# A new merge table for two interleaved groups of boards, and a new lag between them

## The chip, the core and the metric

The kernel runs on one NeuronCore of a Trainium2 chip. The time is that of the device for one launch, in microseconds (us), and lower is better. The engines are named as in the profile: PE is TensorE's matrix multiply, PEld its weight loads, DVE is VectorE, ACT is ScalarE, POOL is GpSimd, SP is the queue that issues DMAs.

## What is computed

128 boards of 64 squares with 256 features pass through four residual layers. Each begins with a layer norm and a ReLU. Layers 0, 1 and 3 are masked attention, layer 2 is a gated graph layer with a tanh.

```python
h = jnp.maximum(_layernorm(x, axis=-1), 0.0)
x = x + _L0_gnn_ref(h, adj, adj, ...)   # 8 heads, six static masks, two from adj
h = jnp.maximum(_layernorm(x, axis=-1), 0.0)
x = x + _L1_gnn_ref(h, adj, ...)        # 4 heads, mask adj
h = jnp.maximum(_layernorm(x, axis=-1), 0.0)
x = x + _L2_gnn_ref(h, adj, ...)        # below
h = jnp.maximum(_layernorm(x, axis=-1), 0.0)
x = x + _L3_gnn_ref(h, adj, ...)        # as layer 1
...
# attention: softmax(where(mask, q k^T * scale, -big)) v, then Wo and bias
# layer 2:
Wh = jnp.einsum('bni,hoi->bhno', h, W) + bW[None, :, None, :]
e = jnp.einsum('bhno,hop->bhnp', Wh, attn)
A_mat = jnp.tanh(jnp.where(adj[:, None], jnp.einsum('bhnp,bhmp->bhnm', e, Wh), 0.0))
hp = jax.nn.relu(jnp.einsum('bhnm,bhmo->bhno', A_mat, Wh))
ha = cat(hp) @ A_w.T ; hf = h @ fc_w.T
coeff = jax.nn.sigmoid(hf @ g1_w.T + ha @ g2_w.T + gbias)
return hf * coeff + ha * (1.0 - coeff)
```

## The kernel before

A group is four boards, 256 rows. Two groups are in flight, in two sets of buffers called slot 0 and slot 1; in tile names the last digit is the slot (`xn1` is slot 1's). There are 32 groups, so 16 turns of both slots: the first turn is written out, the other 15 are one hardware loop (`passes`, line 321), and the rest of slot 1 follows it. Below, one trip of that loop is a pass.

A group's work is a list of 111 steps, `STEPS`: attention layer 0 (here A0), attention layer 1 (A1), the graph layer (L2), attention layer 3 (A3). Every engine walks the same list and does its share of each step. The steps that matter here:

- `bn`, `stats`, `norm`: the layer norm. DVE takes the statistics (line 928 reads x, then 935 and 938), POOL raises to the power -0.5 (line 405), DVE writes the normalised `xn` (line 946).
- `turn`: PE transposes `xn` (line 500); ACT writes the rounded half `hT` (line 760), DVE the rest (line 960). Each fp32 product is taken as three products of such halves, so a consumer waits for both.
- `q`, `k`, `v`, `scores`; then `mask` and `max` on DVE, the exponentials on ACT (line 785, named `max` there too), `soft` on DVE (lines 1014, 1016). A1 and A3 have two units of softmax each, A0 has four.
- `pt` transposes the probabilities on PE (line 577), ACT copies them (line 792). `pv` multiplies them with v on PE; ACT and DVE write the two halves of `oT` (lines 795, 867). `out` is the output projection; DVE adds x (line 1025).
- L2: `r` (four row terms of the scores; DVE line 1045, then POOL spreads them over a 128x1024 tile `row_terms`, line 410), `e` for four heads (ACT line 813, DVE line 1050), `s2` scores and tanh, `a` (halves of the masked tanh, and their row sums), `ah`, `hp` for four heads, `ha`, `hf`, `hat` (transposes, line 711), `g` and `sum` the gate. In `hat` POOL also adds 128x512 numbers to x (line 418).

The order of the two slots on one engine is written out by hand as a table, `ORDER`. It has a number for every step: after step k of slot 0, so many steps of slot 1 are done. The lag says how many of these, at the start of a turn, still belong to slot 1's previous group. There is a table for PE, ACT, DVE and POOL each; SP has its own fixed order, in which the next `x` of a slot is loaded when `res` says that A3's `out` has been added (line 1025). Waits are on semaphores, so any order that doesn't deadlock gives the same numbers, and PE executes its list strictly as it stands. No planner decides anything when the kernel runs.

Within a pass, slot 0's L2 runs beside slot 1's A0, and slot 1's L2 beside slot 0's A0; the A1 of one slot runs beside the A3 of the other. "First half" is from slot 0's A0 `turn` to slot 1's A0 `turn` (slot 1 finishes its L2 and A3 in it), "second half" the rest of the pass.

Of the kernel before, what the change touches and what calls it, by code (L numbers as in the profile page):

```python
# [58 lines left out]
def constants():  # L59
# [22 lines left out]
    for part in (0, LO):  # L82
# [11 lines left out]


ORDER = {
# [5 lines left out]
    "act": (44, (  # L102
# [4 lines left out]
    "dve": (49, (  # L107
# [4 lines left out]
    "pool": (41, (  # L112
# [4 lines left out]
}  # L117


# [1017 lines left out]
```

## Time and profile before

| | |
|---|---|
| median of three runs | 2304.79 us (2302.14 to 2306.58) |
| the profiled execution, as timed | 2314.06 us |
| its span in the trace | 2311.9 us |
| PE busy in the span | 2106.4 us, 91% |
| PEld, DVE, ACT, POOL busy | 81%, 63%, 50%, 8% |
| mean granted TensorE clock | 0.979 of full speed |

The profiled execution is 9.3 us longer than the median of the runs, of which 2.2 us lie outside its span. The table of the span by slices shows PE at nine tenths or more nearly throughout; only the first slices (weights and their products are set up, about 100 us) and the last (one slot alone) have less. A busy PE is an upper figure: the matmuls overlap and their ends are modelled. Idle time before a group is put down to whatever ended it, and "issue" means that the profile shows nothing that was waited for.

### The profile page before, as it was taken

How to read it: one execution, taken by the hardware profiler on the slowest of the kernel's cores; microseconds unless marked ns; L12 is line 12 of the kernel's file. 1: busy time of each engine (PE TensorE's matmuls, PEld its weight loads, DVE VectorE, ACT ScalarE, POOL GpSimd, SP SyncE). 2: the span in 40 equal slices, each digit the busy share in tenths (PEclk: the TensorE clock that was granted, in tenths of full speed). 3: DMA queues.
4: the chain of work that ended last, by engine and by line, in shares of the span. 5: the costliest groups of instructions: out<-in, count | busy, mean ns of one | idle time of the engine just before them, and what ended most of it. 6: DMA issues, size and time to landing. Idle time of an engine off the chain costs nothing.

```text
span 2311.9 us, 53587 instructions
## 1 busy us (share of the span) xinstructions
PE 2106.4 (91%) x21228; PEld 1875.6 (81%) x21228; DVE 1466.1 (63%) x3769; ACT 1160.4 (50%) x3862; POOL 192.5 (8%) x203
## 2 busy tenths in 40 slices
PE   6799999999999999999999999999999999999997
PEld 5688888888887888888888887888888888888886
DVE  4466666666666666667666666666667666666663
ACT  3355454455454555455455455455455455455452
POOL 0000101100101100101100100110100100100100
PEclk8799999999999999999999999999999999999998
DMA  5000000000000000000000000000000000000000
GB/s 169 1 9 5 11 12 11 12 11 2 12 11 12 10 11 3 11 12 11 12 11 2 12 11 12 11 11 3 11 12 11 12 11 2 12 11 12 10 6 5
DMA packets 40644, 30.89 MB, mean 13 GB/s; under 512 B 15664, under 2 KB 40240, under 8 KB 40432
## 3 DMA queue, kind: packets, MB, share of 16 engines
q1 hardware_dynamic: 40432, 27.48, 4.1%
q8 instruction: 204, 3.34, 0.6%
q14 instruction: 8, 0.07, 0.0%
HBM read 19.08 MB, written 8.39 MB: 12 GB/s over the span
## 4 chain that ended last, share of the span: by engine, by line
PE 71%; DVE 11%; ACT 11%; issue 4%; DMA 3%; POOL 1%; SPq 0%; DVEq 0%; POOLq 0%; ACTq 0%
PE ps L432 66%; ACT probs L785 5%; PE ps L577 3%; DVE xn L946 2%; PE ps L500 2%; DMA x<-x 2%; DVE wide L1050 2%; ACT oT L795 1%; DVE small L928 1%; DVE probs L1016 1%; ACT probsT L792 1%; DVE aT L867 1%; ACT hT L760 1%; POOL small L405 1%; DMA raw_mats<-mats 1%
## 5 line engine op out<-in xcount | busy, mean ns | idle before, releaser
L432 PE MATMUL ps<-hT,w_hi 128*128 128x256 f32 x2560 | 499.0, 288 | 9.8 <-ACT hT L760 9.6
L432 PEld LDWEIGHTS ps<-hT,w_hi 128*128 128x128 f32 x2560 | 409.5, 190 | 24.8 <-ACT hT L760 18.4
L785 ACT ACTIVATE probs<-probs,small 128x64 f32<-128x64 f32 x1024 | 341.4, 338 | 77.6 <-DVE small L1006 76.2
L432 PE MATMUL ps<-hT,w_lo 128*128 128x256 f32 x1280 | 336.6, 283 | 0.0
L432 PE MATMUL ps<-w_hi,hT 128*128 128x256 f32 (+1 forms) x1024 | 249.0, 312 | 0.0
L432 PEld LDWEIGHTS ps<-hT,w_lo 128*128 128x128 f32 x1280 | 243.6, 190 | 2.0
L432 PE MATMUL ps<-wide,w_hi 128*128 128x256 f32 x1024 | 218.3, 287 | 3.1
L432 PE MATMUL ps<-w_hi,oT 128*128 128x256 f32 x768 | 187.5, 309 | 31.3 <-DVE oT L867 17.0
L405 POOL TENSOR_TENSOR small<-small,consts 128x2 f32<-128x2 f32 x128 | 88.8, 694 | 1420.7 <-DVE small L938 1420.7
L785 ACT ACTIVATION_READ_ACCUMULATOR probs<-probs,small 128x1 f32 x1024 | 195.2, 191 | 0.0
L432 PEld LDWEIGHTS ps<-w_hi,hT 128*128 128x128 f32 x1024 | 174.9, 188 | 8.4
L432 PE MATMUL ps<-w_hi,cT 128*128 128x256 f32 x768 | 169.3, 298 | 10.9 <-ACT cT L845 8.2
L432 PEld LDWEIGHTS ps<-wide,w_hi 128*128 128x128 f32 x1024 | 164.3, 188 | 17.1 <-ACT wide L830 12.5
L432 PEld LDWEIGHTS ps<-w_hi,oT 128*128 128x128 f32 x768 | 143.8, 203 | 41.2 <-DVE oT L867 40.4
L867 DVE TENSOR_TENSOR oT<-ps,oT 128x256 fp32r<-128x256 f32 x192 | 80.9, 424 | 151.5 <-ACT oT L795 149.4
L760 ACT ACTIVATE hT<-ps 128x256 fp32r<-128x256 f32 x256 | 85.4, 382 | 135.1 <-PE ps L500 134.4
L813 ACT ACTIVATE wide<-ps,c_vec 128x256 fp32r<-128x256 f32 x256 | 107.5, 471 | 88.5 <-PE ps L432 88.5
L432 PEld LDWEIGHTS ps<-w_hi,cT 128*128 128x128 f32 x768 | 126.6, 188 | 28.5 <-ACT cT L845 15.8
L432 PE MATMUL ps<-w_lo,hT 128*128 128x256 f32 (+1 forms) x512 | 149.6, 309 | 0.0
L432 PEld LDWEIGHTS ps<-kT,qT 64*64 64x64 f32 (+1 forms) x4096 | 125.3, 133 | 24.2 <-issue 15.4
L432 PE MATMUL ps<-kT,qT 64*64 64x64 f32 (+1 forms) x4096 | 142.8, 222 | 0.0
L946 DVE TENSOR_SCALAR xn<-x,small 128x256 f32<-128x256 f32 x256 | 120.8, 513 | 23.7 <-POOL small L405 22.5
(123 smaller groups left out, 4454.7 us busy)
## 6 DMA issues: line engine op xcount, KB each, us to landing
raw_mats<-mats SPq DMA_DIRECT2D x8, 1024.0 KB, 11.9
x<-x SPq DMA_DIRECT2D x32, 256.0 KB, 2.9
out<-xn SPq DMA_DIRECT2D x32, 256.0 KB, 3.1
adj<-adjq SPq DMA_DIRECT2D x64, 16.0 KB, 2.0
adjT<-adjt SPq DMA_DIRECT2D x64, 8.0 KB, 2.1
raw_consts<-board_consts SPq DMA_DIRECT2D x1, 451.5 KB, 3.2
raw_rows<-rows SPq DMA_DIRECT2D x1, 256.0 KB, 4.5
bias_cols<-cols SPq DMA_DIRECT2D x1, 6.0 KB, 3.9
```

The costliest lines, as they stand in the source:

```text
L405: nc.gpsimd.tensor_tensor(RSTD[s], VE[s], HALF.broadcast_to([P, TT]), ALU.pow).then_inc(sm["rstd"], 1)
L432: return nc.tensor.matmul(o, lhsT, rhs, start=start, stop=stop, skip_group_check=True)
L500: last = nc.tensor.transpose(bank(s, H_BANKS[c])[:, t * P:t * P + P], XN[s][:, t * D + c * P:t * D + c * P + P], IDENT)
L577: last = nc.tensor.transpose(bank(s, 1 - i)[:, at:at + P], PR[s][:, j, at:at + P], IDENT)
L760: fn(HT[s][:, 0, c, :], bank(s, H_BANKS[c])[:, 0:TOK], ACT.Relu).then_inc(S[s]["hT_hi"], 1)
L785: last = fn(p, p, ACT.Exp, bias=ROWMAX[s][:, row:row + 1], accum_out=ROWSUM[s][:, row:row + 1])
L792: fn(PTS[s][:, j, at], bank(s, 1 - i)[:, at], ACT.Copy).then_inc(sm["pt_sb"], 1)
L795: fn(OT[s][:, 0, i, :].rearrange("p (t e q) -> p t e q", t=TT, e=2), o_view(s, i), ACT.Copy).then_inc(sm["oT_hi"], 1)
L813: last = fn(e_view(s, 0, oc, i), e_bank(s, E_BANKS[i], oc), ACT.Identity, bias=CVEC[:, oc, i:i + 1])
L867: return tt(o, full, hi.bitcast(F32), ALU.subtract)
L946: ts(XN[s][:, t * D:t * D + D], X[s][:, t * D:t * D + D], MV[s][:, t, 0:1], RSTD[s][:, t:t + 1], ALU.subtract, ALU.mult).then_inc(S[s]["xn ...
L1050: stt(e_view(s, 1, oc, i), e_bank(s, E_BANKS[i], oc), CVEC[:, oc, i:i + 1], e_view(s, 0, oc, i).bitcast(F32), ALU.add, ALU.subtract).then_ ...
```

## The change

The four tables of `ORDER` and their lags are replaced; nothing else is touched. Lags go from 44, 44, 49, 41 (PE, ACT, DVE, POOL) to 50, 48, 48, 51. A row of the table as an example; the other rows change in the same manner.

```diff
 ORDER = {
-    "pe": (44, (
-        0, 0, 0, 0, 0, 0, 2, 0, 0, 1, 0, 0, 0, 3, 0, 0, 0, 0, 2, 1, 0, 0, 0, 0, 1, 2, 0, 1, 0, 2, 0, 0, 1,
...
+    "pe": (50, (
+        1, 2, 0, 0, 2, 1, 2, 0, 1, 3, 0, 0, 0, 5, 1, 0, 0, 0, 0, 0, 0, 0, 0, 0, 0, 0, 0, 1, 0, 1, 0, 0, 3,
...
```

What it does in a pass, by the steps of each engine's list:

- PE, both halves: L2's `a` for the first tile comes after the other slot's A0 `k` (it was after `v` in the first half and before `k` in the second). In the first half the four A0 `scores` move behind `ah`; in the second they stood there already.
- PE, both halves: A1's `turn` comes before the other slot's `g`, not behind it. In the first half A0's `out` moves ahead of the last `ha`.
- PE, both halves: A3's first `pt` comes before A1's `out` of the other slot. ACT does the first A3 unit of exponentials before A1's `pv`, and DVE does A3's masks, maxima and first `soft` before A1's `pv`.
- The jump of the loop moves in every list. On PE it stood between slot 1's last `e` and slot 0's A0 `turn`; now it stands behind slot 0's last A3 `out`, ahead of slot 1's `r` and `e`. Slot 1's L2 `turn` comes before that last `out`.
- POOL, slot 1: `row_terms` comes behind slot 0's A0 power. In both halves DVE does `r` and the first head of `e` before A0's `bn` of the other slot, and A3's `out` of one slot behind L2's `turn` of the other, not before it.

POOL's list, from the last rows ahead of the loop (0 and 1 are the slots; `small` holds the norm's statistics). Before:

```order
L410 TENSOR_TENSOR row_terms1<-rs1,consts 128x1024
L321 UNCONDITIONAL_BRANCH
L321 ISA
L405 TENSOR_TENSOR small0<-small0,consts 128x2
L418 TENSOR_TENSOR x1<-x1,f1 128x512
```

And now, from the same place:

```order
L321 UNCONDITIONAL_BRANCH
L321 ISA
L405 TENSOR_TENSOR small0<-small0,consts 128x2
L410 TENSOR_TENSOR row_terms1<-rs1,consts 128x1024
L404 REGISTER_ALU
```

Slot 1's `row_terms` has moved across the jump and stands right behind the power of slot 0's norm, as slot 0's stands behind slot 1's in the middle of the pass (unchanged).

DVE's list in the middle of a pass, from slot 0's L2 `norm`. Before:

```order
L946 TENSOR_SCALAR xn0<-x0,small0 128x256 x2
L1025 TENSOR_TENSOR xn1<-ps,x1 128x256 x2
L960 SCALAR_TENSOR_TENSOR hT0<-ps,hT0 128x256 x2
L928 BN_STATS small1<-x1 128x6
L1044 REGISTER_ALU
L1045 SCALAR_TENSOR_TENSOR rs0<-ps,s0,rs0 4x256
L928 BN_STATS small1<-x1 128x6
L935 BN_AGGR small1<-small1 128x2 x2
L938 TENSOR_SCALAR small1<-small1 128x2
L1050 SCALAR_TENSOR_TENSOR wide0<-ps,c_vec,wide0 128x4x64 x4
L946 TENSOR_SCALAR xn1<-x1,small1 128x256 x2
```

Now:

```order
L946 TENSOR_SCALAR xn0<-x0,small0 128x256 x2
L960 SCALAR_TENSOR_TENSOR hT0<-ps,hT0 128x256 x2
L1025 TENSOR_TENSOR xn1<-ps,x1 128x256 x2
L1044 REGISTER_ALU
L1045 SCALAR_TENSOR_TENSOR rs0<-ps,s0,rs0 4x256
L1050 SCALAR_TENSOR_TENSOR wide0<-ps,c_vec,wide0 128x4x64 x2
L928 BN_STATS small1<-x1 128x6 x2
L935 BN_AGGR small1<-small1 128x2 x2
L938 TENSOR_SCALAR small1<-small1 128x2
L1050 SCALAR_TENSOR_TENSOR wide0<-ps,c_vec,wide0 128x4x64 x2
L946 TENSOR_SCALAR xn1<-x1,small1 128x256 x2
```

A3's `out` of slot 1 and with it the next load of `x1` move behind two `hT0`, and the statistics of `x1` move behind `rs0` and two of the four `wide0`.

PE's list at the end of a pass, from slot 0's second A3 `pt`, as it now is:

```order
L577 MATMUL ps<-consts,probs0 128x128 x2
L585 REGISTER_ALU
L432 MATMUL ps<-probsT0,v0 64x64 x8
...
L432 MATMUL ps<-bias_rows,sel_rows 128x256
L500 MATMUL ps<-consts,xn1 128x128 x4
L432 MATMUL ps<-w_hi,oT0 128x256
...
L321 COMPARE_AND_BRANCH
```

Before, the four transposes of `xn1` stood behind both halves of `out`, `r` and `e` followed them, and the jump came only behind `e`:

```order
L500 MATMUL ps<-consts,xn1 128x128 x4
L432 MATMUL ps<-hT1,u_vec 36x256 x6
...
L432 MATMUL ps<-hT1,w_hi 128x256 x2
L321 REGISTER_ALU
L321 COMPARE_AND_BRANCH
```

## Rows read from the trace of the kernel before

**Rows 1.** The page: engine, busy us, share, instructions; clock by slices.

```profile
PE 2106.4 (91%) x21228; PEld 1875.6 (81%) x21228; DVE 1466.1 (63%) x3769; ACT 1160.4 (50%) x3862; POOL 192.5 (8%) x203
...
PEclk8799999999999999999999999999999999999998
```

**Rows 2.** Stretches: busy us of each engine, granted clock, DMA share, GB/s.

```profile
core 0: us, PE busy (x) PEld busy (x) DVE busy (x) ACT busy (x) POOL busy (x), PEclk, DMA share, GB/s
870.55:1008.31 137.76, 127.42 (x1317) 113.63 (x1317) 90.13 (x235) 71.25 (x240) 11.87 (x12) 1.00 0.04 10
591.99:731.85 139.86, 130.19 (x1317) 116.23 (x1317) 90.54 (x236) 71.24 (x240) 11.89 (x12) 0.98 0.04 10
...
718.87:722.28 3.41, 2.94 (x14) 2.94 (x14) 1.95 (x6) 0.38 (x1) 0.69 (x1) 0.50 0.00 0
715.46:718.87 3.41, 2.18 (x40) 1.33 (x38) 2.80 (x12) 2.23 (x11) 0.00 (x0) 1.00 0.00 0
```

**Rows 3.** PE's waits, pass 870.55 to 1008.31: waiter, releaser, us, times, longest.

```profile
PE ps L500 <- issue: 3.2, 2, 1.7
PE ps L577 <- DVE probs L1016: 2.5, 5, 0.9
PE ps L500 <- DVE xn L946: 1.2, 1, 1.2
```

**Rows 4.** The loop's line: duration ns min/median/max, first and last start.

```profile
L321 PEldq COMPARE_BRANCH  x15: 83/3498/3848, 311.8 to 2250.0; - x15
...
L321 PEldq COMPARE_BRANCH  x1: 3498/3498/3498, 1004.6 to 1004.6; - x1
```

**Rows 5.** PE in order of time (start, us, what, idle before), around the jump.

```profile
999.93 1.10 PE L432 MATMUL ps<-hT,u_vec 128*36 128x256 f32 x6 [0.26 <-ACT hT L760]
...
1006.39 0.40 PE L432 MATMUL ps<-hT,w_hi 128*128 128x256 f32 x2
1008.31 0.56 PE L500 MATMUL ps<-consts,xn 128*128 128x128 f32 x3 [1.52 <-issue]
```

**Rows 6.** POOL and DVE in order of time, in the middle of the pass.

```profile
936.60 0.69 POOL L405 TENSOR_TENSOR small<-small,consts 128x2 f32<-128x2 f32 x1 [7.54 <-DVE small L938]
937.26 1.91 POOL L410 TENSOR_TENSOR row_terms<-rs,consts 128x1024 fp32r<-128x1024 f32 x1
...
972.99 1.28 POOL L418 TENSOR_TENSOR x<-x,f 128x512 f32<-128x512 f32 x1
...
934.53 0.43 DVE L928 BATCH_NORM_STATS2 small<-x 128x6 f32<-128x256 f32 x1 [2.46 <-DMA x<-x]
...
936.56 1.66 DVE L1050 SCALAR_TENSOR_TENSOR wide<-ps,c_vec,wide 128x256 fp32r<-128x256 f32 x4
938.13 1.51 DVE L946 TENSOR_SCALAR xn<-x,small 128x256 f32<-128x256 f32 x2
```

**Rows 7.** ACT and PE, A1 and A3 late in the pass; a group of the page.

```profile
989.82 0.66 ACT L792 ACTIVATE probsT<-ps 128x256 f32<-128x256 f32 x2 [1.05 <-PE ps L577]
...
L785 ACT ACTIVATE probs<-probs,small 128x64 f32<-128x64 f32 x1024 | 341.4, 338 | 77.6 <-DVE small L1006 76.2
...
991.75 0.39 PE L432 MATMUL ps<-w_hi,oT 128*128 128x256 f32 x1 [0.65 <-DVE oT L867]
...
995.36 0.44 PE L577 MATMUL ps<-consts,probs 128*128 128x128 f32 x2 [0.89 <-DVE probs L1016]
...
997.31 0.39 PE L432 MATMUL ps<-w_hi,oT 128*128 128x256 f32 x1 [0.47 <-ACT oT L795]
```

**Rows 8.** PE in order of time: `hat`, `g`, and behind them A1's `q`.

```profile
973.34 0.60 PE L711 MATMUL ps<-consts,f 128*128 128x128 f32 x4
974.19 0.39 PE L432 MATMUL ps<-w_hi,cT 128*128 128x256 f32 x1 [0.26 <-ACT cT L845]
...
977.31 0.39 PE L432 MATMUL ps<-hT,w_hi 128*128 128x256 f32 x1 [0.31 <-ACT hT L760]
```

**Rows 9.** PE in order of time: `a` of the second tile, first half.

```profile
881.36 1.05 PE L432 MATMUL ps<-aT,sel_rows 128*128 128x512 f32 x2
```

More of the change, by code:

```diff
@@ L96 @@
 ORDER = {
[5 rows of a table removed]
-    "act": (44, (
[4 rows of a table removed]
-    "dve": (49, (
[4 rows of a table removed]
-    "pool": (41, (
[4 rows of a table removed]
[5 rows of a table added]
+    "act": (48, (
[4 rows of a table added]
+    "dve": (48, (
[4 rows of a table added]
+    "pool": (51, (
[4 rows of a table added]
 }
```

30 rows, old and new, of the table ORDER are left out of this document.

## The prediction

> **What bounds the kernel now.** Read the page first. PE is busy 91% of the span [rows 1], no other engine passes 81%, and PE's own work is the same before and after: the change only permutes it. So the question is how much of PE's idle time goes or comes. Next take one pass of the loop that ran at full clock, 870.55 to 1008.31: 137.76 us with PE busy for 127.42 [rows 2]. About 10.3 us of idle time per pass, times 15 passes, is all that an order can win: 155 us at the very most. The waits of that pass [rows 3] say where it lies: ahead of transposes of `xn` (3.2 and 1.2 us), ahead of transposes of probabilities (2.5 us), and in a dozen waits of 0.2 to 0.7 us for halves of `hT`, `oT` and `cT`. Then I read these places in order of time, with ACT, DVE and POOL beside PE. Of each place I ask how long the chain that ends the wait is, and how much PE work the new order puts over it. Three facts of the trace carry what follows.
>
> First, the jump of the loop is dear on PE alone. It took 3.5 us in the median (15 times, the 83 ns is the last, which is not taken) [rows 4]. In this pass it began at 1004.6, while the last matmul before it began at about 1006.5, and PE went on at 1008.31 after 1.52 us idle [rows 5]. So the sequencer was some 2.2 us ahead of its engine and hid that much of the jump. The matmuls in that stretch follow each other every 0.12 us, so it was ahead by about 18 of them, or 36 instructions with their weight loads.
>
> Second, `norm` on DVE is held up by POOL. `row_terms` ran from 937.26 to 939.17; the two `norm` issued at 938.13 took 1.51 us together where 0.74 is the rule, and the first ended only when POOL had ended [rows 6]. By itself one takes 0.41.
>
> Third, the clock. In the pass 591.99 to 731.85 it fell twice, and the pass took 139.86 instead of 137.76 us [rows 2]: 1.05 us for each fall. Before the fall at 718.87 PE had done 40 short matmuls with gaps, 2.18 us busy of 3.41; then the clock was 0.50, that is 1.2 instead of 2.4 GHz. I count 11 such falls in the 15 passes.
>
> **The change part by part**, per pass, minus is a gain.
>
> (a) `a`, `ah`, `scores`, `hp`. In the first half the second `a` took 1.05 us [rows 9] where 0.63 would do, and `hp` waited some 0.65 us behind `ah` for the halves of `ah`'s result. The new order puts 64 small matmuls (1.9 us) over the second wait. It shortens the cover of the second `a` from the scores (1.9 us) to `v` (14 matmuls of 0.12, 1.7 us); against it stand a copy of the row sums, one of `aT` (0.6 each) and DVE's half (0.7), so about 0.3 us stay open. In the first half the exponentials of A0 now stand before `hp`'s first ReLU on ACT (4 x 0.338 = 1.35 us [rows 7]), and `ha` pays 0.35 of it. First half -0.5. In the second half the first `a` loses a wait of 0.5 us and gets the 0.3 of the second: -0.3. Sum **-0.8** (bounds -1.4 and 0).
>
> (b) `turn` before `g`. Now PE waits 0.26 behind `hat`, then runs `g`, `turn`, waits 0.31, and reaches `q` 3.97 us after `hat` (973.34 to 977.31) [rows 8]. After: `norm` in this place is itself held by POOL's addition (972.99 to 974.27 [rows 6]), so `turn` starts about 1.1 us after `hat`; its four transposes and `g` (1.6 us) then cover every copy, and `q` starts after 3.4. Second half -0.55. In the first half `norm` came after the addition and `q` after 3.49 us; it now takes the second half's form: -0.1. Sum **-0.65** (-1.0 to -0.2).
>
> (c) A3's first `pt` between A1's `pv` and `out`, first half. ACT starts A3's exponentials right behind the two copies of rows 7 (989.82 + 0.66) instead of behind A1's `pv`, 1.4 us earlier, but A1's `pv` copies now wait 1.35 us for them, so PE idles 1.45 us ahead of A3's `pt` instead of 0.65 ahead of A1's `out` (991.75). In exchange the second `pt` loses its 0.89 (995.36) and the whole chain to L2's `r` ends 0.7 us sooner: **-0.7** (-1.2 to 0).
>
> (d) The middle of the pass. DVE now adds A3's `out` of slot 1 after two `hT`, which sends the load of `x1` 1.0 to 1.9 us later, and does `rs` and two `wide` before `bn`. `bn` starts 1.45 us later than the 934.53 of rows 6, with 0.5 less between it and the power. The power ends 0.95 us later, `row_terms` follows it at once as now, and `norm`, with only two `wide` between, meets it whole: its first half ends with `row_terms`, near 940.3 on that pass's clock, not 939.5. PE waited 1.2 us here [rows 3] and will wait about 2.1: **+0.9** (0 to +1.5).
>
> (e) The end of the pass. Slot 0's A3 has the pattern of (c), but DVE has `bn` and `stats` of L2 before A3's `pv`; I find A3's first `out` starting 7.6 us after A1's `pt` (989.34), where it is 7.97 (997.31 [rows 7]). Then PE waits 0.4 us for `xn1`, does `turn` and the second `out` (1.2 us). The sequencer has 36 instructions from that first `out` to the jump, so it reaches the jump as `out` begins, and `r` can start 3.5 + 0.2 us later: 11.4 us after `pt`, where `r` at 999.93 came after 10.59 [rows 5]. That is +0.8 up to here. Behind `e` the jump's 1.52 us are gone, but POOL now does slot 1's `row_terms` (1.92 us) between the power and `norm`. The power ends 6.4 us after `r`, `row_terms` 8.3, and PE's A0 `turn` starts 8.45 after `r`; it was 1008.31 - 999.93 = 8.38. What the jump gave back the hold takes. Sum **+0.85** (-0.6 to +2.1).
>
> The sum is -0.8 - 0.65 - 0.7 + 0.9 + 0.85 = -0.4 us per pass, 15 passes: -6 us. The clock: sparse stretches on PE around A1 and A3 get longer but fewer. I take as many falls as now, but they come to lie over `out`'s dense matmuls at 14 x 0.12 more, 0.3 us dearer: +3 us (0 to +12). The first turn and the tail have one slot alone on PE and keep their order: 0. So the profiled 2311.9 would be 2309, and the median of 2304.8 becomes **2302 us**. A measurement of this kernel tells about 0.2% (4.6 us) from no change.
>
> On (d) and (e) the Trainium skill bears, page SBUF — State Buffer, section "SBUF: two separate sides": the port pair that VectorE and GpSimd share is an exclusive lock, and whichever starts first holds it for its whole instruction. By this rule the 1.92 us are lost whole. The trace agrees, with 15 of 15 `norm` under `row_terms` lengthened from 0.41 to 1.19. On the jump in (e), the Trainium skill's page TensorE: Matmul & The Clock Gate, "Architectural detail: the array is 16× 32×32, not 1× 128×128", gives TensorE's queue a depth of 64. By that, the sequencer would be 32 matmuls or 3.8 us ahead and today's jump would be hidden whole; the trace shows 2.2 us ahead and 1.52 open, so the measurement decides.
>
> **The rivals.** *The hold does not come about (faster).* If DVE's `norm` gets in before `row_terms`, (d) turns from +0.9 to about -0.6 and (e) from +0.85 to about -0.5: with the rest -3.2 per pass, 2260 us. For it: POOL's start and DVE's lie only 0.1 us apart. Against it: the same pair with the addition of line 418 in place of `row_terms` starts 0.08 us apart, and there POOL was first in 16 of 16. *The fills count in full (faster).* (a) to (c) reach 0.3 us more each, or (e) comes out even: -1.3 per pass, 2286 us. For it: DVE and ACT are idle 37% and 50%. *The jump lies bare (slower).* If the sequencer does not run past the wait for `xn1`, it reaches the jump only 8.9 us after `pt`, and `r` starts after 12.6 instead of 11.4: +1.2 per pass, and with the longer gap a fall of the clock in every second pass. That gives +0.8 per pass plus 4 to 6 us: 2321 us. It decides from the point where less than 3.5 us of PE work stands between the sequencer's arrival at the jump and the last matmul ahead of it; now there are 2.2, then 2.4 with a wait inside. *The order doesn't reach the end at all:* each gain is eaten by the next wait of the same pass, 2305.
>
> **How the numbers follow.** The sum as worked, 2302 with its own range of 2292 to 2312: 0.45, of which 0.18 faster by over 0.2%, 0.22 within, 0.05 slower. The jump bare: 0.22. Fills in full: 0.15. No hold: 0.10. Nothing: 0.08. Faster 0.43, same 0.30, slower 0.27. The range 2280 to 2325 leaves out the no-hold case and the far end of the bare jump.
>
> **What would show it.** PE's idle ahead of line 500 in the middle of a pass at 2 us (d), and again at 1.3 to 1.6 before slot 0's, put down to `xn` and no longer to "issue". DVE's `norm` at 2.0 us under `row_terms` 30 times instead of 1.19 15 times. The jump still 3.5 us, with some 1.2 us open ahead of `r`. No wait of `q` for `hT` behind `g`, no 0.89 ahead of the second A3 `pt`, one of 1.4 ahead of the first. The prediction is wrong if POOL's `row_terms` doesn't meet `norm`, or if PE's idle ahead of `r` is over 2.5 us.

## The result, and the profile after

| | before | after |
|---|---|---|
| median | 2303.47 us (2301.18 to 2306.58, 4 runs) | 2340.77 us (2337.04 to 2342.48, 4 runs) |
| the profiled execution, as timed | 2314.06 us | 2341.77 us |
| its span | 2311.9 us | 2339.6 us |
| mean granted TensorE clock | 0.979 | 0.964 |

The changed kernel takes 1.0159 times as long as the kernel before, with a 95% interval of 1.0140 to 1.0177: **slower by 1.6%**, and outside the predicted range of 2280 to 2325.

First the page of the kernel after, its lines of busy times and of the chain, and two groups (line, engine, shape, count, busy us, mean ns, idle before it). They answer to [rows 1].

```profile
PE 2096.4 (90%) x21228; PEld 1890.3 (81%) x21228; DVE 1502.8 (64%) x3769; ACT 1145.4 (49%) x3862; POOL 190.7 (8%) x203
...
PE 71%; DVE 14%; issue 8%; ACT 4%; POOL 2%; DMA 1%; DVEq 0%; SPq 0%; ACTq 0%; POOLq 0%
...
L946 DVE TENSOR_SCALAR xn<-x,small 128x256 f32<-128x256 f32 x256 | 169.8, 704 | 45.6 <-POOL small L405 41.4
L500 PE MATMUL ps<-consts,xn 128*128 128x128 f32 x512 | 108.9, 306 | 84.0 <-DVE xn L946 84.0
```

PE has the same 21228 matmuls as before. DVE is busy 37 us longer: line 946, the `norm` that POOL holds up, grew by 49 us (from 120.8 to 169.8), and the rest of DVE's work is 12 us shorter. The span grew by 27.7 us; the medians lie 37.3 apart. The profiled execution of before was 9.3 us above the median known then, so the traces explain 27 of the 37 us; for the other 10 there is no trace of a typical execution of the kernel before.

PE's waits inside the loop (180 to 2230 us; waiter, releaser, us in total, times, longest), first the kernel before:

```profile
PE ps L577 <- DVE probs L1016: 37.0, 73, 0.9
PE ps L500 <- issue: 21.9, 14, 1.8
PE ps L432 <- ACT hT L760: 15.2, 53, 0.3
```

and after:

```profile
PE ps L500 <- DVE xn L946: 64.7, 58, 2.0
PE ps L577 <- DVE probs L1016: 40.8, 29, 1.4
PE ps L432 <- issue: 37.1, 28, 2.6
```

This is the heart of the case. Before, idle time is spread over many waits of at most 1.2 us, but for the 14 of 1.3 to 1.8 us that the jump leaves ahead of slot 0's A0 `turn`. Now the 29 waits for probabilities are 1.4 us each, those for `xn` ahead of A0's `turn` reach 2.0 us, and the bare jump of 2.2 to 2.6 us stands in every pass (14 of the 28 put down to "issue"; the others are of 0.3 us).

Next the places of the prediction. The middle of a pass, POOL, DVE and PE in order of time, answering to [rows 6]:

```profile
947.82 0.69 POOL L405 TENSOR_TENSOR small<-small,consts 128x2 f32<-128x2 f32 x1 [7.74 <-DVE small L938]
948.47 1.91 POOL L410 TENSOR_TENSOR row_terms<-rs,consts 128x1024 fp32r<-128x1024 f32 x1
...
948.62 2.23 DVE L946 TENSOR_SCALAR xn<-x,small 128x256 f32<-128x256 f32 x2
...
950.59 1.22 PE L500 MATMUL ps<-consts,xn 128*128 128x128 f32 x4 [1.98 <-DVE xn L946]
```

`row_terms` starts right behind the power, and the pair of `norm` takes 2.23 us instead of 0.74. The end of the pass (PE, and the loop's line), answering to [rows 4, 5, 7]:

```profile
1001.21 0.66 PE L577 MATMUL ps<-consts,probs 128*128 128x128 f32 x4
...
1008.76 0.38 PE L432 MATMUL ps<-w_hi,oT 128*128 128x256 f32 x1 [0.87 <-DVE oT L867]
...
1009.70 0.79 PE L500 MATMUL ps<-consts,xn 128*128 128x128 f32 x4
...
1013.61 0.90 PE L432 MATMUL ps<-hT,u_vec 128*36 128x256 f32 x6 [2.28 <-issue]
...
1021.83 0.87 PE L500 MATMUL ps<-consts,xn 128*128 128x128 f32 x4 [1.63 <-DVE xn L946]
...
L321 PEldq COMPARE_BRANCH  x1: 3354/3354/3354, 1010.1 to 1010.1; - x1
```

The sequencer reached the jump at 1010.1, 8.9 us behind A1's `pt`, 1.34 us behind the first matmul of A3's `out` (1008.76, which had waited for `oT`) and 0.4 us behind the start of `turn`, and PE stood idle for 2.28 us. Last, stretches of PE with the granted clock as seventh figure (us, busy of each engine, clock, DMA share, GB/s), behind the waits for `xn` of three halves, and one just behind the first of them, answering to [rows 2]:

```profile
882.70:886.10 3.40, 3.40 (x9) 2.58 (x8) 2.79 (x8) 0.60 (x1) 0.00 (x0) 0.50 0.02 5
886.10:889.50 3.40, 3.40 (x27) 3.22 (x26) 1.56 (x3) 1.12 (x2) 0.00 (x0) 1.00 0.00 0
950.90:954.30 3.40, 3.40 (x11) 2.81 (x11) 3.09 (x8) 0.38 (x1) 0.00 (x0) 0.51 0.00 0
1022.60:1026.00 3.40, 3.40 (x10) 2.65 (x10) 2.63 (x7) 0.89 (x3) 0.00 (x0) 0.50 0.02 5
```

PE was never idle in the first, third and fourth, but ran `s2` at 1.2 GHz: 9 to 11 matmuls, where an experiment below has 14 of them in such a stretch with 0.35 us to spare. The clock record of the trace has **31 such falls between the first and the last A0 `turn` of the loop, where the kernel before has 11**. Of the 31, 18 begin within 1.4 us of A0's `turn`, 6 around A3's first `pt` and 7 around the bare `r`. Of the 11 before, ten begin 1.5 to 2.7 us behind the second A3 `pt`, which waits 0.89 us among other short waits, and only one behind the 14 waits of 1.3 to 1.8 us at the jump. So the length of a wait does not decide by itself.

### Where the time went

I cut each half of a pass at five marks on PE: A0's `turn`, `hat`, A1's `pt`, `r` and the next A0's `turn`. Of each piece I took the median over those of the loop's 15 or 14 halves in which the clock did not fall, in us:

| piece | before, first half | after | before, second half | after | term |
|---|---|---|---|---|---|
| A0's `turn` to `hat` | 34.48 | 33.92 | 33.96 | 33.86 | (a) |
| `hat` to A1's `pt` | 15.52 | 15.30 | 16.01 | 15.32 | (b) |
| A1's `pt` to `r` | 10.71 | 9.78 | 10.58 | 12.40 | (c), (e) |
| `r` to A0's `turn` | 7.88 | 8.70 | 8.42 | 8.20 | (d), (e) |
| sum | 68.59 | 67.70 | 68.97 | 69.78 | |

At full clock a pass takes 137.56 before and 137.48 us after: the new order by itself changes nothing. The 14.5 passes between the marks would take 1994.4 and 1992.4 us; they took 2007.4 and 2034.4. What is left over is 13.0 us for 11 falls and 42.0 us for 31 falls, 1.2 and 1.35 us each. So -2 us are the order and +29 us the clock, together the 27 us by which the two traces differ.

### The profile page after: what moved, and what is told of

Read it like the earlier page. It is cut to its first block, busy times and chain, and to the rows that moved or that the text cites. A ratio compares the mean times of both kernels' runs of the same rounds, so it can differ in the third digit from the quotient of the medians.

```text
span 2339.6 us, 53632 instructions
## 1 busy us (share of the span) xinstructions
PE 2096.4 (90%) x21228; PEld 1890.3 (81%) x21228; DVE 1502.8 (64%) x3769; ACT 1145.4 (49%) x3862; POOL 190.7 (8%) x203
## 4 chain that ended last, share of the span: by engine, by line
PE 71%; DVE 14%; issue 8%; ACT 4%; POOL 2%; DMA 1%; DVEq 0%; SPq 0%; ACTq 0%; POOLq 0%
PE ps L432 65%; DVE xn L946 4%; PE ps L500 4%; PE ps L577 2%; DVE small L928 2%; ACT probs L785 2%; POOL small L405 2%; DVE x L1025 1%; DVE aT L867 1%; DVE rs L867 1%; DVE small L935 1%; DVE wide L1050 1%; ACT rs L826 1%; ACT probsT L792 1%; DVE probs L1016 1%
## 5 line engine op out<-in xcount | busy, mean ns | idle before, releaser
L432 PE MATMUL ps<-hT,w_hi 128*128 128x256 f32 x2560 | 493.5, 287 | 0.2
L432 PE MATMUL ps<-wide,w_hi 128*128 128x256 f32 x1024 | 212.3, 284 | 0.2
L946 DVE TENSOR_SCALAR xn<-x,small 128x256 f32<-128x256 f32 x256 | 169.8, 704 | 45.6 <-POOL small L405 41.4
L500 PE MATMUL ps<-consts,xn 128*128 128x128 f32 x512 | 108.9, 306 | 84.0 <-DVE xn L946 84.0
L432 PE MATMUL ps<-w_hi,cT 128*128 128x256 f32 x768 | 159.9, 290 | 0.3 <-ACT cT L845 0.3
L500 PEld LDWEIGHTS ps<-consts,xn 128*128 128x128 f32 x512 | 59.6, 144 | 120.0 <-DVE xn L946 111.3
```

Of the source, the lines that this page charges most:

```text
L432: return nc.tensor.matmul(o, lhsT, rhs, start=start, stop=stop, skip_group_check=True)
L500: last = nc.tensor.transpose(bank(s, H_BANKS[c])[:, t * P:t * P + P], XN[s][:, t * D + c * P:t * D + c * P + P], IDENT)
L946: ts(XN[s][:, t * D:t * D + D], X[s][:, t * D:t * D + D], MV[s][:, t, 0:1], RSTD[s][:, t:t + 1], ALU.subtract, ALU.mult).then_inc(S[s]["xn ...
```

## The experiments

The kernels ran in three groups, each on one chip and with the kernel before beside it, which took 2312.9 to 2315.5 us there; ratios are to that. The changed kernel itself ran only on the first chip, beside 2303.5 us, so between it and the others the traces are the safer comparison: they give somewhat less than the ratios (31 and not 39 us from the changed kernel to a_pejump). All kernels do the whole computation. "Full clock" is the sum of the table above made for that kernel, for 14.5 passes (before 1994.4, after 1992.4), "falls" are counted as above. The expectations count them over a slightly longer stretch: 32, 28 and 17 for the changed kernel, a_pejump and a_both. a_fill has no full-clock sum, because in every one of its second halves the clock falls around `r`.

| kernel | ratio (95% interval) | full clock | traced | falls |
|---|---|---|---|---|
| after | 1.0159 (1.0140 to 1.0177) | 1992.4 | 2034.4 | 31 |
| a_pejump | 0.9991 (0.9970 to 1.0013) | 1964.7 | 2003.2 | 27 |
| a_rtfirst | 0.9914 (0.9887 to 0.9941) | 1954.1 | 1990.0 | 25 |
| a_both | 0.9751 (0.9723 to 0.9778) | 1932.0 | 1952.0 | 14 |
| a_both_ptfill | 0.9673 (0.9657 to 0.9689) | 1934.7 | 1935.6 | 1 |
| b_rtlate | 1.0013 (0.9996 to 1.0030) | 1994.5 | 2008.1 | 10 |
| b_rtfirst | 0.9999 (0.9986 to 1.0012) | 1995.6 | 2007.5 | 8 |
| b_ab | 0.9918 (0.9901 to 0.9934) | 1968.0 | 1991.6 | 17 |
| b_c2 | 1.0011 (0.9992 to 1.0030) | 1992.6 | 2013.4 | 19 |
| b_c | 1.0079 (1.0051 to 1.0106) | 1997.3 | 2022.6 | 23 |
| b_pejump | 1.0088 (1.0056 to 1.0120) | 2011.6 | 2028.9 | 12 |
| a_fill | 1.0087 (1.0065 to 1.0108) | none | 2028.2 | 20 |
| a_pejump_fill | 1.0073 (1.0050 to 1.0096) | 2000.4 | 2027.9 | 15 |

### The jump: a_pejump and b_pejump

a_pejump is the changed kernel with five steps of PE moved back across the jump:

```diff
-    "pe": (50, (
-        1, 2, 0, 0, 2, 1, 2, 0, 1, 3, 0, 0, 0, 5, 1, 0, 0, 0, 0, 0, 0, 0, 0, 0, 0, 0, 0, 1, 0, 1, 0, 0, 3,
+    "pe": (45, (
+        0, 0, 0, 0, 0, 1, 2, 0, 1, 3, 0, 0, 0, 5, 1, 0, 0, 0, 0, 0, 0, 0, 0, 0, 0, 0, 0, 1, 0, 1, 0, 0, 3,
...
-        0, 0, 5, 0, 0, 0, 2, 4, 0, 0, 2, 0)),
+        0, 0, 5, 0, 0, 0, 2, 4, 0, 0, 2, 5)),
```

> The changed kernel with the loop's jump of PE alone put back behind slot 1's last e (lag 50 to 45, five steps L2 r and e0 to e3 moved back across the jump); ACT, DVE, POOL and the order of PE's steps stay as changed. Theory A (the clock): the extra 36 us of the changed kernel are mostly its 32 falls of the granted clock instead of 11, of which about 7 begin at r behind the bare jump. PE's idle ahead of r falls from 3.9 to under 1.5 us, the hold of xn by row_terms stays at both halves: 1.0 us per pass for the idle and 7 falls at 1.65 us, so 2341 - 15 - 12 = 2314 us with some 25 falls. Theory B (idle time alone; falls cost nothing since they lie beside waits): 2341 - 15 = 2326 us whatever the count of falls. Theory C (the order of A1 and A3, not the jump, costs the time): 2336 to 2341 us.

Measured 0.9991, 1.7% below the changed kernel by the ratios and 31 us by the traces; I had expected 27. The same place, and the loop's line:

```profile
985.44 0.66 PE L577 MATMUL ps<-consts,probs 128*128 128x128 f32 x4
...
995.42 0.86 PE L432 MATMUL ps<-hT,u_vec 128*36 128x256 f32 x6
...
1003.74 0.90 PE L500 MATMUL ps<-consts,xn 128*128 128x128 f32 x4 [1.76 <-DVE xn L946]
...
L321 PEldq COMPARE_BRANCH  x1: 3578/3578/3578, 999.8 to 999.8; - x1
```

`r` follows `pt` after 9.98 us instead of 12.40, and the jump ends at 1003.4, under the wait for `xn` that is there anyway. The full-clock sum is 27.7 us shorter, and four falls are gone.

b_pejump is the reverse: the kernel before, with only PE's jump moved ahead of `r`.

```diff
-    "pe": (44, (
-        0, 0, 0, 0, 0, 0, 2, 0, 0, 1, 0, 0, 0, 3, 0, 0, 0, 0, 2, 1, 0, 0, 0, 0, 1, 2, 0, 1, 0, 2, 0, 0, 1,
+    "pe": (50, (
+        6, 0, 0, 0, 0, 0, 2, 0, 0, 1, 0, 0, 0, 3, 0, 0, 0, 0, 2, 1, 0, 0, 0, 0, 1, 2, 0, 1, 0, 2, 0, 0, 1,
...
-        0, 0, 0, 0, 1, 12, 0, 0, 1, 0, 0, 8)),
+        0, 0, 0, 0, 1, 12, 0, 0, 1, 0, 0, 2)),
```

> The kernel before with the loop's jump of PE alone moved ahead of slot 1's r (lag 44 to 50, L2 r and e0 to e3 behind the jump); all else as before. The jump then lies behind the transposes of xn1 and is bare. Theory A: idle ahead of r grows by 1.5 us, the 1.52 us ahead of slot 0's A0 turn shrinks by 0.9, so +0.6 us per pass, +9 us, and the clock falls at r in every second pass, 7 x 1.05 = 7 us: 2305 + 16 = 2321 us with 16 to 20 falls. Theory B (idle time alone): 2314 us. Theory C (the place of the jump makes no difference, its 3.5 us only change places): within 3 us of 2305.

Measured 1.0088 (1.0056 to 1.0120), 20 us; theory A had 1.007, B 1.004 and C 1.000.

```profile
1008.16 0.39 PE L432 MATMUL ps<-w_hi,oT 128*128 128x256 f32 x1 [0.47 <-ACT oT L795]
...
1009.92 0.60 PE L500 MATMUL ps<-consts,xn 128*128 128x128 f32 x4
1013.06 1.49 PE L432 MATMUL ps<-hT,u_vec 128*36 128x256 f32 x6 [2.54 <-issue]
...
L321 PEldq COMPARE_BRANCH  x1: 3451/3451/3451, 1009.4 to 1009.4; - x1
```

`r` comes 12.86 us behind `pt` (at 1000.20), 2.3 us later than before. At full clock `r` to A0's `turn` is 2.0 us shorter in exchange (6.42 us, from the two passes without a fall there), but A0's `turn` to `hat` behind it is 0.7 us longer, which I can't explain. The full-clock sum is 17 us above the kernel before, of the 21.5 us between the two traces. The loop has 12 falls where the kernel before has 11, and they now begin around `r`. So most of what the jump costs here is idle time and not the clock.

### The hold: a_rtfirst, b_rtlate, b_rtfirst

a_rtfirst is the changed kernel with POOL's `row_terms` ahead of the other slot's A0 power, in both halves:

```diff
-        0, 0, 0, 0, 0, 0, 0, 1, 0, 2, 0, 0, 0, 0, 0, 1, 0, 4, 0, 3, 0, 0, 0, 1, 0, 0, 0, 0, 0, 0, 0, 0, 0,
-        0, 0, 0, 1, 0, 0, 5, 0, 3, 0, 0, 0, 0, 0, 0, 3, 0, 27, 0, 0, 0, 0, 0, 0, 2, 1, 2, 0, 29, 0, 0, 3, 0,
+        0, 2, 0, 0, 0, 0, 0, 0, 0, 1, 0, 0, 0, 0, 0, 1, 0, 4, 0, 3, 0, 0, 0, 1, 0, 0, 0, 0, 0, 0, 0, 0, 0,
+        0, 0, 0, 1, 0, 0, 5, 0, 3, 0, 0, 0, 0, 0, 0, 3, 0, 27, 0, 0, 0, 0, 0, 0, 2, 0, 0, 0, 32, 0, 0, 3, 0,
```

> The changed kernel with POOL's row_terms ahead of the power of the other slot's A0 norm, in both halves; nothing else. norm is then no longer held by row_terms. Theory A (the clock): xn comes about 0.85 us sooner, 30 times, 26 us, and the some 20 falls of the clock that begin right behind the wait ahead of A0's turn go with their idle time, 20 x 1.65 = 33 us: 2341 - 26 - 33 = 2282 us, with some 12 falls. Theory B (idle time alone): 2341 - 26 = 2315 us. Theory C (row_terms only changes places with the power, which then comes as much later): within 5 us of 2341, and PE's waits ahead of line 500 stay near 2 us.

Measured 0.9914, 44 us below the changed kernel by the traces and already faster than the kernel before.

```profile
923.22 1.92 POOL L410 TENSOR_TENSOR row_terms<-rs,consts 128x1024 fp32r<-128x1024 f32 x1 [3.86 <-DVE rs L1045]
927.02 0.69 POOL L405 TENSOR_TENSOR small<-small,consts 128x2 f32<-128x2 f32 x1 [1.88 <-DVE small L938]
...
928.29 0.87 PE L500 MATMUL ps<-consts,xn 128*128 128x128 f32 x4 [0.41 <-DVE xn L946]
```

Here nobody meets anybody: `row_terms` has ended 1.88 us before the power can begin, and `r` to A0's `turn` goes from 8.70 to 7.34 us in the first half and from 8.20 to 6.72 in the second. The 18 falls behind this wait are gone, all of them. But 31 became only 25, not the 12 I expected: 17 now begin around A3's first `pt` instead of 6, and 8 around the bare `r` instead of 7. The gain is idle time, 38 us at full clock, more than theory A's 26, and 6 us of clock.

b_rtlate puts only slot 1's `row_terms` across the jump in the kernel before (the first of POOL's rows; the last two change with it):

```diff
-    "pool": (41, (
-        0, 1, 0, 0, 0, 0, 1, 0, 2, 1, 0, 0, 0, 1, 0, 0, 1, 0, 0, 1, 0, 0, 0, 2, 0, 0, 0, 0, 0, 3, 0, 0, 6,
+    "pool": (50, (
+        0, 0, 10, 0, 0, 0, 1, 0, 2, 1, 0, 0, 0, 1, 0, 0, 1, 0, 0, 1, 0, 0, 0, 2, 0, 0, 0, 0, 0, 3, 0, 0, 6,
...
```

b_rtfirst moves only slot 0's ahead of the power:

```diff
-        0, 11, 0, 0, 0, 0, 0, 0, 4, 0, 0, 0, 0, 0, 0, 2, 0, 0, 0, 0, 2, 1, 0, 1, 0, 7, 0, 2, 2, 0, 2, 0, 0,
+        0, 11, 0, 0, 0, 0, 0, 0, 4, 0, 0, 0, 0, 0, 0, 2, 0, 0, 0, 0, 2, 1, 0, 1, 0, 3, 0, 0, 8, 0, 2, 0, 0,
```

> The kernel before with slot 1's row_terms on POOL moved across the jump, behind the power of slot 0's A0 norm (POOL's lag 41 to 50); all else as before. norm of slot 0 is then held by row_terms as slot 1's is in the middle. Theory A: PE's jump covers the hold, since power ends 6.4 us and row_terms 8.3 us after r, and A0's turn started 8.38 us after r anyway: +0.1 us per pass, 2306 us (2303 to 2310), falls 11 to 14. Rival: the hold adds to the jump, +1.0 us per pass and a fall in every second pass at A0's turn: 2305 + 15 + 8 = 2328 us.

> The kernel before with POOL's row_terms of slot 0 ahead of the power of slot 1's A0 norm in the middle of the pass; nothing else. norm in the middle is then held by nobody. Theory A: r to A0's turn 7.74 us in the middle becomes 7.1 to 7.3 (the changed kernel went from 8.70 to 7.34), 15 times 0.5 us and no more falls: 0.9965 of the kernel before. Theory B (the wait ahead of A0's turn is set by the load of x1 and bn, not by norm): 1.000.

Measured 1.0013 and 0.9999. The first is as theory A had it: behind `e` the jump of 3.5 us covers the hold. In the second theory A failed (it had 0.9965). In the kernel before, `row_terms` ahead of the power gains nothing:

```profile
933.60 1.91 POOL L410 TENSOR_TENSOR row_terms<-rs,consts 128x1024 fp32r<-128x1024 f32 x1 [6.14 <-DVE rs L1045]
935.62 0.69 POOL L405 TENSOR_TENSOR small<-small,consts 128x2 f32<-128x2 f32 x1
...
934.40 1.13 DVE L938 TENSOR_SCALAR small<-small 128x2 f32<-128x2 f32 x1
```

The hold has only changed its place: DVE's line 938, which writes what the power needs, starts at 934.4, beside `row_terms`, takes 1.13 us instead of 0.17 and ends with it, and the power follows then. The old order does the first `bn` before `r`, the new one `r` and the first `e` before `bn`. In a_rtfirst, with the new order on DVE, POOL is idle for 1.88 us between `row_terms` and the power. So it is the change's own part (d) that makes the room for `row_terms`; the change only left `row_terms` on the wrong side of the power.

### Both at once: a_both

Its edits are the two shown of a_pejump and a_rtfirst, on PE:

```diff
-    "pe": (50, (
+    "pe": (45, (
...
```

and the two rows of POOL's table.

> The changed kernel with both parts undone that were undone one by one so far: PE's jump back behind slot 1's last e, and POOL's row_terms ahead of the power in both halves. One by one they gave 0.9991 and 0.9914 of the kernel before, where the changed kernel had 1.0159. Theory A (they add up, since the jump lengthens the way to r and the hold the way to A0's turn): 1.0159 - 0.0168 - 0.0245 = 0.975, some 2256 us on a chip that gives 2313 for the kernel before. Theory B (behind e the jump's 3.5 us cover the hold in the second half, so only the first half's share of the hold comes on top): 1.0159 - 0.0168 - 0.012 = 0.987, some 2283 us.

Measured 0.9751 (2254.9 beside 2312.9 us), as theory A had it: the two losses nearly add up. At full clock they give 60 us together, and 28 and 38 alone.

### Keeping PE's clock: a_fill, a_pejump_fill, a_both_ptfill

a_fill is the changed kernel with useless work ahead of the wait of A0's `turn`:

```diff
             def transposed_h(s, a, c, v):
+                for _ in range(10 if a == 0 and c == 0 else 0):
+                    mm(bank(s, 1)[:, 0:D], WHI[:, 0, 0, 0:P], WHI[:, 0, 0, :], True, True)
                 for t in range(TT):
```

> The changed kernel with ten more matmuls of 256 columns on PE (1.2 us) ahead of A0's turn of each slot, that is ahead of the wait for xn of about 2 us; they write to a bank that nobody reads, so the result is the same. Theory A (the clock falls because PE idles here): the some 20 of 32 falls that begin right behind this wait go, at about 1.5 us each: 1.0159 - 0.013 = 1.003 of the kernel before, with 12 to 15 falls left (those around r and pt). Theory B (falls cost nothing, or come whatever PE does here): 1.016 to 1.018, falls near 32 or, if they go, without a gain.

Measured 1.0087 (1.0065 to 1.0108), below the changed kernel by 0.7% in the ratios and 6 us in the traces. Theory A had foreseen 1.3%. The middle of a pass, and the clock behind it, to be held against the rows of the kernel after:

```profile
947.16 1.35 PE L432 MATMUL ps<-w_hi 128*128 128x256 f32 x10
949.35 0.87 PE L502 MATMUL ps<-consts,xn 128*128 128x128 f32 x4 [0.84 <-DVE xn L948]
...
949.00:952.40 3.40, 3.05 (x14) 2.26 (x15) 3.37 (x10) 0.78 (x2) 0.14 (x1) 1.00 0.00 0
```

The chain is the same: `norm` is held as long, and A0's `turn` starts 8.89 us behind `r` instead of 8.70. PE only did nothing useful in place of nothing. Yet the clock is 1.00 behind it, where it was 0.51. No fall begins there in any of the 29 halves, where 18 of 29 had one, and the piece up to A0's `pt` takes 24.3 instead of 25.7 us in the median. 31 falls became 20. The matmuls also cost something: 0.19 us ahead of `turn` in the first half and 0.26 ahead of `r` in the second, 6 us in all at full clock. So the 11 falls gave back some 12 us, 1.1 each. What kept the gain small is that the falls around the bare `r` rose from 7 to 14, one in every pass.

a_pejump_fill has the same ten matmuls in a_pejump.

> As a_pejump (the changed kernel with PE's jump back behind e, 0.9991 of the kernel before, 28 falls of the clock in the loop, of which about 20 begin behind the wait for xn ahead of A0's turn), with ten more matmuls of 256 columns (1.2 us) ahead of that wait, into a bank that nobody reads. Theory A (idle ahead of A0's turn makes the clock fall, a fall costs about 1.5 us): 0.9991 - 0.012 = 0.987, with some 8 to 12 falls left. Theory B (falls cost nothing or don't depend on this wait): 0.999 to 1.001. Where the jump already covers the wait (second half) the matmuls may cost up to 1.2 us x 15 instead: then 0.995.

Measured 1.0073 (1.0050 to 1.0096), 0.8% **slower** than a_pejump although its falls went from 27 to 15. Neither theory had it. In the second half the new matmuls stand right behind the jump:

```profile
1008.83 0.40 PE L432 MATMUL ps<-hT,w_hi 128*128 128x256 f32 x2
1011.04 1.43 PE L432 MATMUL ps<-w_hi 128*128 128x256 f32 x10 [1.81 <-issue]
1014.34 1.12 PE L502 MATMUL ps<-consts,xn 128*128 128x128 f32 x4 [1.87 <-issue]
```

After the jump's 1.81 us they run, and then PE idles once more for 1.87 us with nothing awaited; DVE had `xn` by 1011.2. `r` to A0's `turn` took 11.4 us there, not 8.6. This idle time outweighs the falls; and seven of the 15 falls lasted 6.83 us here, all others of the loop 3.41. The trace has a likely cause for the second gap in the queue that loads instructions (`q8`, 1005 to 1016 us):

```profile
q8 instruction: 3, 0.05, 2.5%
```

Two of these three transfers, of 16 KB each, start at 1008.05 and 1011.63; the jump ends 1.3 us behind the end of the first, and PE goes on 1.3 us behind the end of the second. In all 14 passes of this kernel the second gap ends 1.2 to 1.6 us behind the end of such a second transfer. No run tests it. a_pejump has a second transfer at the same distance from the jump and no gap, so it may be the place of the added instructions in the program, and not the matmuls as such, that costs.

a_both_ptfill puts them elsewhere, into a_both ahead of the 1.4 us wait for A3's first probabilities:

```diff
                 elif k == "pt":
+                    for _ in range(10 if a == 2 and i == 0 else 0):
+                        mm(bank(s, 2)[:, 0:D], WHI[:, 0, 0, 0:P], WHI[:, 0, 0, :], True, True)
                     for u, _, j, cj in turned(a)[i]:
```

> As a_both (0.9751 of the kernel before, 17 falls of the clock in the loop, most of them beginning behind the waits of 0.35 and 1.41 us around A1's and A3's pt), with ten more matmuls of 256 columns (1.2 us) on PE ahead of the 1.41 us wait for A3's first probabilities, into a bank that nobody reads. Theory A (this idle time makes the clock fall there, and a fall costs 1.4 us even where nothing else changes): falls 17 to about 4, 0.9751 - 0.008 = 0.967, some 2237 us where the kernel before has 2313. Theory B (the falls stay, or go without a gain): 0.975 to 0.977.

Measured 0.9673 (2238.8 us), as theory A had it. Two lines of its page and the cores:

```profile
core 0: 2235.3 us, clock 0.986
...
PE 2087.7 (93%) x21548; PEld 1890.6 (85%) x21548; DVE 1457.5 (65%) x3769; ACT 1145.2 (51%) x3862; POOL 192.3 (9%) x203
```

This is the cleanest measure of the clock's price, some 1.5 us per fall. The full-clock sum is 2.7 us *longer* than a_both's, one fall is left of 14, and the loop is 16.4 us shorter. It is the fastest kernel of the study, 3.3% below the kernel before.

### The parts (a), (b) and (c) by themselves

b_ab is the kernel before with (a) and (b) on all four engines, of which PE's first row:

```diff
-        0, 0, 0, 0, 0, 0, 2, 0, 0, 1, 0, 0, 0, 3, 0, 0, 0, 0, 2, 1, 0, 0, 0, 0, 1, 2, 0, 1, 0, 2, 0, 0, 1,
+        0, 0, 0, 0, 0, 0, 2, 0, 1, 3, 0, 0, 0, 5, 1, 0, 0, 0, 0, 0, 0, 0, 0, 0, 0, 0, 0, 1, 0, 1, 0, 0, 3,
...
```

> The kernel before with parts (a) and (b) alone, as in the changed kernel, in both halves: on PE L2's a, ah and A0's v and scores, and A1's turn ahead of g, with the steps of ACT, DVE and POOL that belong to them; A1 to A3, the middle and the end of the pass are those of before. The prediction took -0.8 and -0.65 us per pass: A0's turn to F (hat) 0.8 shorter over both halves, F to A3's turn 0.65 shorter. The changed kernel's marks show F to A3's turn 0.38 and 0.90 shorter and the way to F about 0.6 and 0.1 shorter: theory A, -1.5 to -2.0 us per pass, and since the sparse stretch behind hat gets denser the falls of the clock stay at 8 to 14: 2313 - 26 = 2287 us, 0.989 of the kernel before. Theory B (the next wait of the pass eats it): 0.997 to 1.0.

Measured 0.9918 (0.9901 to 0.9934), where theory A had 0.989. At full clock it gains 26 us, the 1.5 to 2.0 per pass of theory A, and its 17 falls instead of 11 (I had expected 8 to 14) take 10 us of that back.

b_c and b_c2 are the kernel before with (c); b_c2 also moves A3's second `soft` on DVE and A3's `v` on ACT. PE's edit is the same in both:

```diff
-        0, 2, 2, 0, 1, 4, 0, 0, 2, 0, 0, 2, 0, 0, 0, 3, 0, 0, 0, 1, 1, 2, 2, 0, 4, 3, 0, 1, 0, 1, 0, 0, 0,
+        0, 2, 2, 0, 1, 4, 0, 0, 2, 0, 0, 2, 0, 0, 0, 3, 0, 0, 0, 7, 0, 0, 0, 0, 3, 3, 0, 1, 0, 1, 0, 0, 0,
...
-        0, 0, 0, 0, 1, 12, 0, 0, 1, 0, 0, 8)),
+        0, 0, 0, 0, 1, 7, 5, 0, 1, 0, 0, 8)),
```

> The kernel before with part (c) alone, in both halves: on PE A3's first pt ahead of A1's out of the other slot, on ACT the first unit of A3's exponentials ahead of A1's pv, on DVE A3's maxima and first soft ahead of A1's pv. Theory A (what the changed kernel's marks show, P to r 0.6 to 0.9 us shorter, A3's turn to P 0.2 longer): -1.1 us per pass, -17 us, and some 7 more falls of the clock at 1.5 us, +10: 0.997 of the kernel before with some 18 falls. Theory B (no more falls): 0.9925. Theory C (A1's pv pays on ACT what A3's pt gains): 1.000.

> The kernel before with part (c) alone, this time whole: as b_c, and in addition A3's second soft ahead of A1's out on DVE and A3's v copy ahead of A1's pt on ACT, as in the changed kernel. b_c measured 1.0079 with P to r 1.3 us longer, where I had expected 0.9 shorter; its second A3 pt came 3.4 us behind the first, where the changed kernel has 2.1. Theory A (the soft behind out was the fault, (c) itself gives what the changed kernel shows): P to r 0.6 to 0.9 us shorter than before in each half, A3's turn to P 0.2 longer: -1.1 us per pass less some 10 falls at 1.4 us, 0.997 to 0.999. Theory B ((c) needs the rest of the new order, by itself it costs): 1.005 to 1.01.

Measured 1.0079 and 1.0011; theory A had 0.997 for b_c and at most 0.999 for b_c2. At full clock b_c is 3 us longer than before, with waits ahead of A3's `pt` of 1.4 and 1.9 us in the two halves and twelve falls more. b_c2 is 2 us shorter, nothing like 16, and has eight falls more. The group of A3's and A1's `pt` in b_c2, waits of PE in the loop:

```profile
PE ps L577 <- DVE probs L1016: 48.4, 44, 1.5
```

Before it was 37.0 us in 73 waits of at most 0.9. So (c) by itself hardly shortens the way; it lays several short waits together into one of 1.4 to 1.5 us, and the clock falls around it. In the changed kernel A1's `pt` to `r` is 0.93 us shorter in the first half all the same. The traces show where: two waits of b_c2, of 0.39 and 0.88 us at full clock, are none and 0.34 us there, together 0.93 us. Beside (c) the changed kernel has DVE do A1's `soft` before A3's `k`, and A3's first `pv` before it finishes the statistics of L2. That this order is the reason is read from the traces; no run has it alone. Two lines of b_c2 and one of the kernel after:

```profile
916.08 0.44 PE L577 MATMUL ps<-consts,probs 128*128 128x128 f32 x2 [0.39 <-DVE probs L1016]
...
923.39 0.39 PE L432 MATMUL ps<-w_hi,oT 128*128 128x256 f32 x1 [0.88 <-DVE oT L867]
...
1079.50 0.39 PE L432 MATMUL ps<-w_hi,oT 128*128 128x256 f32 x1 [0.34 <-DVE oT L867]
```

## Why the prediction was wrong

**The failed step is the clock.** "I take as many falls as now" stood on nothing but the sparse stretches around A1 and A3. I had seen that the change lengthens three waits, to 2.1, 1.45 and some 1.3 us, and did not ask what they do to the clock, though the fall that I quoted, at 718.87, stood behind just such a stretch. The waits themselves came about as foretold (medians of 1.85 and 1.6 us ahead of A0's two `turn`, 1.4 ahead of `pt`), except the one ahead of `r`. The term was +3 us (0 to +12); it is +29: 31 falls instead of 11. The price per fall was right for the kernel before (1.05 forecast, 1.2 measured) and is 1.35 in the kernel after. One of my own rivals had the mechanism, "with the longer gap a fall of the clock in every second pass", but only for one of three places.

On this the Trainium skill says, page TensorE: Matmul & The Clock Gate, section "A second HAM failure mode: psum-queue depth-cycling", that short idles of PE between groups of matmuls can make its clock go down and up again and cost throughput between bursts. The trace agrees, with 31 falls where PE is 90% busy. I had not weighed that page against the change.

**(a)** -0.66 per pass, forecast -0.8. **(b)** -0.91, forecast -0.65, within its bounds; b_ab shows both alone, -1.8 together. **(c)** -0.93, forecast -0.7: right in size, wrong in its reason. b_c2 shows that the swap I described gives next to nothing by itself; the gain stands in two waits that the neighbouring order on DVE seems to shorten, which no run shows alone.

**(d)** +0.82, forecast +0.9. `norm` met `row_terms` 31 times, at 1.91 us per instruction in the mean, as foretold. This is the page SBUF — State Buffer of the Trainium skill again, section "SBUF: two separate sides", by which the one of the two that comes second is blocked until the other's whole instruction is over; 2.23 us for the pair instead of 0.74 agrees. The rival without a hold did not come about, and a_rtfirst shows that its price was right: 1.36 and 1.48 us in the two halves, where I had 1.5 and 1.35.

**(e)** +1.60, forecast +0.85, within its bounds of -0.6 to +2.1, and the second failed step. I let the sequencer run 36 instructions ahead of `out`, past the waits for `oT` and `xn1`, and begin the jump as `out` begins. It began the jump 1.33 us behind `out`'s first matmul, in 14 of 14 passes, 8.9 us behind `pt`, and `r` came after 12.4. These are the figures of the rival "the jump lies bare" (8.9 and 12.6, where the forecast was 11.4), at a chance of 0.22; its 2321 us fell short because it, too, added seven falls and not twenty. But that rival blamed the wait for `xn1`, and b_pejump speaks against it: there the transposes wait for nothing and start 0.5 us after the jump does, and the jump still begins 1.3 us behind the first `out` matmul that waited for `oT`, with the same 36 instructions between. So the sequencer seems to have been held at `oT`, and the rival's figures came out right partly by luck.

The sum of the five is -0.08 per pass, forecast -0.4: -2 us instead of -6. The order was sized well in sum, partly because (e) missed by 0.75 one way and (a) to (c) gained 0.35 more than forecast the other way, and the answer was missed by the clock. Undone, the bare jump gives 27.7 us of the loop at full clock (a_pejump, which comes out even, 0.9991), and the hold by `row_terms` 38 us (a_rtfirst). So the change held a much better order than the one measured.

## What to carry to other kernels

- Where PE is the bound, an order is to be judged by the length of its waits and not by their sum alone. Two orders with the same full-clock time differed by 29 us, and one of them had laid its idle time together into waits of 1.4 to 2.6 us. What runs around the wait counts too: behind the 14 waits of 1.3 to 1.8 us of the kernel before the clock fell once. Length is what to look at first, and the clock record of the trace decides.
- In this kernel the loop's jump belongs behind dense work and ahead of a wait that is there anyway (a_pejump), not behind a wait and ahead of the next work (b_pejump, 0.9% slower).
- Where a wait can't be shortened, useless matmuls ahead of it hold the clock and may pay (0.8% in a_both_ptfill). Right behind the jump they cost 0.8% in the one kernel that had them there.

## What the hardware showed that I had not expected

- How far PE's sequencer is ahead depends on what stands before. Behind `e`, in dense work, it began the jump 2.2 us before PE ran out of work [rows 5]; with a wait of PE for `oT` 36 instructions before the jump it was 1.2 us (after) and 1.1 us (b_pejump), in all 14 passes of each. It reads as if the sequencer does not pass a wait that isn't met yet; no run varies this alone.
- The jump takes 3347 ns in the median on PE's sequencer, and 45 on ACT's, 56 on DVE's and 45 on POOL's, in the same kernel (the loop's line of the kernel after; min/median/max ns, first and last start us):

```profile
L321 PEldq COMPARE_BRANCH  x15: 83/3347/3657, 306.1 to 2272.8; - x15
L321 ACTq COMPARE_BRANCH  x15: 40/45/45, 313.3 to 2276.3; - x15
L321 DVEq COMPARE_BRANCH  x15: 50/56/67, 314.2 to 2277.2; - x15
```

The Trainium skill's page Advanced Engine Details and Errata, section "Control Flow Timing", gives about 108 ns for a compare-and-branch. The other engines stay below it, PE's is thirty times as long; here the measurement decides.

- The jump's length follows a load of instructions. In each of the 14 kernels and in each of the 14 jumps that are taken, one 16 KB transfer of the instruction queue starts 0.9 to 1.6 us after the jump began and takes 0.9 to 1.5 us, and the jump ends 1.3 to 1.6 us behind its end. During the last jump of the loop, which isn't taken and takes 83 ns, none starts.
- Ten matmuls more behind the jump opened a second gap of up to 1.9 us with nothing awaited (a_pejump_fill), which ends behind a second such transfer. That this is its cause is likely and not shown.
- A fall of the clock cost 1.1 to 1.5 us in these kernels, less than the 1.7 us that half speed over such a stretch of 3.4 us would take, probably because part of it lies beside waits.
